# A two-layer convolution kernel: the next load of x moved between the halves of the store, and another order of calls in the first unit

## The chip, the core and the metric

The kernel runs on one core of one Trainium2 chip. The metric is the device time of the whole kernel in microseconds (us), lower is better. The core has five engines that run their own instruction lists and meet only at semaphores: TensorE (PE), VectorE (DVE), ScalarE (ACT), GpSimd (POOL) and SyncE (SP), which here only issues transfers.

## What is computed

The input x is (4, 256, 64, 64), batch, channels, rows, columns. Layer 0 makes 49 attention weights for each pixel from a 7x7 convolution with dilation 2 and a 1x1 convolution behind it, and applies them to the 49 shifted copies of x. Layer 1 adds a gelu term and normalises over the channels.

```python
k = lax.conv_general_dilated(x, w1, window_strides=(1, 1), padding=[(6, 6), (6, 6)], rhs_dilation=(2, 2), dimension_numbers=DN) + b1[None, :, None, None]
k = lax.conv_general_dilated(k, w2, window_strides=(1, 1), padding=[(0, 0), (0, 0)], dimension_numbers=DN) + b2[None, :, None, None]
attn = jax.nn.softmax(k, axis=1)
x = jnp.einsum('bkchw,bkhw->bchw', shifts, attn)          # shifts: the 49 shifted x
y = jax.nn.gelu(yc.T[None, :, None, :] + x * D[None, :, None, None], approximate=False)
out = x + y                                               # then layer norm over the channels
```

yc comes from a scan of 64 steps over a state of 32.

## The kernel before

Dilation 2 lets even and odd rows be treated apart, so the work is cut into 8 units: 4 images times 2 row parities. A unit n is the 32 rows of one parity, with 256 channels as two halves of 128 partitions. x of an even unit lies in raw0, of an odd one in raw1.

The weights are joined first: composite(g) multiplies w2 (relative to the last tap) into row g of w1 on TensorE (14 of them), ScalarE copies five rows in each half (copy_row), VectorE forms sums of rows (row_sums). The convolution over rows is a fast scheme with few products: differences and sums of rows of x (make_u1, make_x1_plus and so on; four of them, c1, c0, c2 and w, on GpSimd) give 11 arrays. Each array is scaled and split in a high fp16 part on ScalarE (v_high) and a low one on VectorE (v_low), into a ring of four slots; the combined weights likewise (weights_high and weights_low, 26 set halves of two instructions each on VectorE). conv(n, first, last) does steps first to last - 1 of 49 on TensorE, 20 matmuls each, seven steps to a block. A block begins only when its arrays are there; in unit 0 (cold) also when its weights are:

```python
if d % DSTEPS == 0:
    pe.wait_ge(vlo, ARRAYS * n + BLOCK_ARRAYS[b])
    if cold:
        pe.wait_ge(w_low, 2 * BLOCK_PARTS[b])
```

The arrays wanted by the seven blocks are 2, 4, 6, 8, 9, 10 and 11, the set halves 4, 8, 12, 16, 20, 24 and 26. The fifth block also waits for the third logit step, the sixth for the fourth.

x is also turned on TensorE (turn_x, eight calls a unit), copied with scale by ScalarE (turned_x) and its low part taken by VectorE (turned_x_low), through two PSUM banks, so turning g waits for low part g - 2. While unit n is convolved, the engines finish unit m = n - 1: logits_i, logits_0 and two turnings of the logits (turn_logits, line 457), softmax, the spread of the attention to bands (spread, line 478), the product of bands and turned x (apply, line 495), gelu, mean and variance, and scale_shift, which completes an output piece and raises the semaphore affine. All orders are written out by hand in each engine's list; an engine that waits blocks what is behind it.

The scale of a unit needs the largest |x|: ScalarE takes it for each half (bound), GpSimd over the partitions (amax), VectorE makes the scales from it (scales). In unit 0 the maximum goes another way, over TensorE.

SP issues the loads and stores. In unit n it waits for the four GpSimd rows and the eight turnings of the old x, loads x of unit n + 1 into the other buffer's place, then stores the four pieces of the unit before (q is the half of the rows, h of the channels) as scale_shift completes them. The pieces with q = 0 are completed late in unit n, those with q = 1 early in unit n + 1. VectorE takes up the new x in make_u1(n + 1) (line 1028), which waits for raw_in.

## Time and profile before

| | |
|---|---|
| median of three runs | 895.67 us (894.84 to 896.17) |
| the profiled execution, device time | 896.21 us |
| its span in the trace | 894.4 us |
| TensorE busy | 803.0 us (90%) |
| VectorE busy | 722.4 us (81%) |
| ScalarE busy | 519.9 us (58%) |
| GpSimd busy | 188.4 us (21%) |
| mean granted TensorE clock | 0.947 |

Times in the trace count from the span's start. Busy time is an average over stages: the first 148 us are the first unit with the weights, then units 1 to 7 follow, and from about 819 us the last unit is finished without a convolution beside it.

### The profile page before, as it was taken

What the parts mean: (1) busy time and instruction counts of PE and PEld (TensorE: products, weight loads), DVE (VectorE), ACT (ScalarE), POOL (GpSimd) and SP (SyncE); (2) the same over time, 40 slices, a digit from 0 to 9 for tenths busy, and PEclk for the clock granted to TensorE, in tenths of its full rate; (3) what the DMA queues carried; (4) which work ended last, traced back from release to release, by engine and by line L of the source; (5) the groups of instructions that cost most, each with busy time, mean ns of one, the idle gap of its engine ahead of it and who ended that gap; (6) DMA issues with size and microseconds to landing.
All of it is one profiled execution on the core that took longest, in us unless ns stands there. A gap on an engine that the chain in (4) does not pass through costs nothing.

```text
span 894.4 us, 27128 instructions
## 1 busy us (share of the span) xinstructions
PE 803.0 (90%) x12261; PEld 493.8 (55%) x12261; DVE 722.4 (81%) x876; ACT 519.9 (58%) x834; POOL 188.4 (21%) x100
## 2 busy tenths in 40 slices
PE   4979787999997999899997999899989999996485
PEld 4975333575555655565564645565546655663451
DVE  3899769889995999689986999599967999677336
ACT  2363232766674666665584767557665659465546
POOL 3114102112510233013311151024301341021010
PEclk9999889999997999999997999999997999999588
DMA  9322005000125010700151011601070011002103
GB/s 312 72 52 45 2 2 95 2 3 2 48 53 92 3 48 2 143 3 1 49 113 33 2 48 42 104 1 40 11 143 2 1 49 50 3 1 64 32 1 94
DMA packets 133597, 41.78 MB, mean 47 GB/s; under 512 B 133145, under 2 KB 133226, under 8 KB 133226
## 3 DMA queue, kind: packets, MB, share of 16 engines
q1 hardware_dynamic: 132248, 40.01, 19.9%
q8 instruction: 96, 1.57, 0.7%
q10 hardware_dynamic: 1234, 0.04, 0.1%
q14 instruction: 19, 0.16, 0.1%
HBM read 23.27 MB, written 16.78 MB: 45 GB/s over the span
## 4 chain that ended last, share of the span: by engine, by line
PE 51%; DVE 15%; issue 12%; ACT 11%; DMA 8%; POOL 1%; SPq 1%; DVEq 0%; ACTq 0%; POOLq 0%
PE cv L438 26%; DMA raw<-in_x_dram 7%; PE wk L495 6%; PE pcomp L603 5%; PE wk L478 4%; PE ms L516 3%; ACT chs L737 3%; ACT V L700 3%; PE wk L529 2%; DVE R L1028 2%; DVE tg L1250 2%; PE wk L457 2%; DVE V L1110 1%; DVE XT L1139 1%; DVE Z L1158 1%
## 5 line engine op out<-in xcount | busy, mean ns | idle before, releaser
L438 PE MATMUL cv<-V,W 128*32 128x496 f16 (+6 forms) x7840 | 447.1, 383 | 19.7 <-issue 7.5
L438 PEld LDWEIGHTS cv<-V,W 128*32 128x32 f16 (+1 forms) x7840 | 201.5, 97 | 224.7 <-issue 41.6
L313 POOL TENSOR_TENSOR R<-raw 128x1152 f32<-128x1152 f32 x32 | 100.2, 3130 | 258.4 <-DVE V L1110 93.8
L700 ACT ACTIVATE V<-R,sc 128x1024 f16<-128x1024 f32 (+1 forms) x88 | 110.5, 1274 | 55.1 <-PE cv L438 54.3
L1110 DVE SCALAR_TENSOR_TENSOR V<-R,sc,V 128x1024 f16<-128x1024 f32 (+1 forms) x88 | 122.4, 1399 | 9.7 <-ACT V L700 9.6
L478 PE MATMUL wk<-AT,sel 128*128 128x16 f16 x2560 | 85.1, 192 | 23.1 <-DVE band L1235 21.2
L495 PE MATMUL wk<-band,XT 128*128 128x224 f16 (+1 forms) x960 | 102.9, 268 | 2.6 <-DVE band L1235 1.4
L478 PEld LDWEIGHTS wk<-AT,sel 128*128 128x128 f16 x2560 | 79.6, 103 | 44.7 <-DVE band L1235 29.6
L495 PEld LDWEIGHTS wk<-band,XT 128*128 128x128 f16 x960 | 83.3, 99 | 25.5 <-issue 5.3
L1235 DVE TENSOR_TENSOR band<-wk,band 128x512 f16<-128x512 f32 x80 | 54.7, 689 | 44.0 <-ACT band L751 43.8
L751 ACT CAST band<-wk 128x512 f16<-128x512 f32 x80 | 46.7, 584 | 69.4 <-PE wk L478 68.4
L731 ACT ACTIVATE XT<-wk,sc 128x512 f16<-128x512 f32 x64 | 42.9, 681 | 53.6 <-PE wk L529 52.9
L760 ACT ACTIVATE o<-wk,sc 128x512 f32<-128x512 f32 x64 | 45.7, 730 | 46.7 <-PE wk L495 46.6
L1041 DVE SCALAR_TENSOR_TENSOR R<-R 128x1024 f32<-128x1024 f32 (+1 forms) x56 | 72.5, 1298 | 0.2
L1028 DVE SCALAR_TENSOR_TENSOR R<-raw 128x512 f32<-128x512 f32 (+1 forms) x48 | 48.2, 1047 | 27.5 <-DMA raw<-in_x_dram 27.4
L1139 DVE SCALAR_TENSOR_TENSOR XT<-wk,sc,XT 128x512 f16<-128x512 f32 x64 | 47.2, 746 | 16.5 <-ACT XT L731 16.3
L338 POOL TENSOR_TENSOR chs<-o 128x1024 f32<-128x1024 f32 x14 | 36.7, 2622 | 110.4 <-DVE o L1256 95.1
L344 POOL TENSOR_TENSOR chs<-tg 128x1024 f32<-128x1024 f32 x14 | 34.5, 2462 | 96.3 <-ACT tg L773 96.3
L603 PE MATMUL pcomp<-w2t,w1raw 128*128 128x48 f32 x196 | 45.0, 418 | 9.4 <-DMA w1raw<-in_L_conv_w_dram 9.4
L1250 DVE SCALAR_TENSOR_TENSOR tg<-o,dcol,yc 128x1024 f32<-128x1024 f32 x32 | 40.4, 1279 | 13.4 <-ACT o L760 13.1
L529 PEld LDWEIGHTS wk<-id,raw 128*128 128x128 f32 x256 | 35.1, 208 | 27.9 <-issue 14.2
L603 PEld LDWEIGHTS pcomp<-w2t,w1raw 128*128 128x128 f32 x196 | 43.7, 312 | 10.0 <-issue 9.6
(138 smaller groups left out, 903.1 us busy)
## 6 DMA issues: line engine op xcount, KB each, us to landing
raw<-in_x_dram SPq DMA_DIRECT2D x16, 1024.0 KB, 11.5
out_dram<-o SPq DMA_DIRECT2D x28, 512.0 KB, 3.9
w1raw<-in_L_conv_w_dram SPq DMA_DIRECT2D x2, 3136.0 KB, 16.8
out_dram<-o SPq DMA_DIRECT2D x8, 256.0 KB, 3.4
cm<-in_L_conv_Cmat_dram ACTq DMA_DIRECT2D x1, 32.0 KB, 8.4
dcol<-in_L_conv_D_dram ACTq DMA_DIRECT2D x2, 0.5 KB, 9.8
lnw<-in_L_conv_ln_w_dram ACTq DMA_DIRECT2D x2, 0.5 KB, 7.2
lnb<-in_L_conv_ln_b_dram ACTq DMA_DIRECT2D x2, 0.5 KB, 7.2
```

What stands on the lines that cost most here:

```text
L313: nc.gpsimd.tensor_tensor(R[buffer][:, :, :, :], rows_of(par, j + 2), rows_of(par, j), ALU.subtract).then_inc(pool_rows, 1)
L438: ins = pe.matmul(to.rearrange("p (w t c) -> p w t c", w=2, c=COLS)[:, :, :, c0:c1], W[:, ws, h * K7 + v, k0:k1], slot(n, a)[:, low, :, t0 ...
L478: ins = pe.matmul(wk[:, r % 2, c * TILES:(c + 1) * TILES].rearrange("p (w j) -> p w j", w=2), sel[:, s, f:f + P], AT[:, :, r:r + 29:4, c], ...
L495: ins = pe.matmul(wk[:, y % 2, (r0 - 16 * q) * COLS:(r1 - 16 * q) * COLS], XT[:, xl, 8 * w + j, h, :], band[:, bl, 8 * w + j, r0 - 4 * j + ...
L603: last = pe.matmul(pcomp[:, g % 3, v * P:v * P + REL], w1h[:, u * K7 + v, :], w2t[:, 0:REL], start=True, stop=True)
L700: nc.scalar.activation(v_array(n, a, 0), array(a), ACT.Identity, scale=sc[:, par, 3:4]).then_inc(vhi, 1)
L1028: nc.vector.scalar_tensor_tensor(out=R[buffer][:, 0:wins, h, :], in0=raw[par][:, h, r:r + 4 * wins - 3:4, :], scalar=-4.0, in1=raw[par][:, ...
L1041: nc.vector.scalar_tensor_tensor(out=part(*out), in0=part(*a), scalar=factor, in1=part(*b), op0=ALU.mult, op1=ALU.add).then_inc(row_made, 1)
L1110: nc.vector.scalar_tensor_tensor(out=v_flat(n, a, 1), in0=array_flat(a), scalar=sc[:, par, 3:4], in1=v_flat(n, a, 0), op0=ALU.mult, op1=AL ...
L1139: nc.vector.scalar_tensor_tensor(out=low, in0=wk[:, g % 2, :], scalar=sc[:, par, 3:4], in1=high, op0=ALU.mult, op1=ALU.subtract).then_inc( ...
L1235: nc.vector.tensor_tensor(band[:, 1, :, r, :], wk[:, r % 2, :].rearrange("p (c t) -> p t c", t=TILES), band[:, 0, :, r, :], ALU.subtract). ...
L1250: nc.vector.scalar_tensor_tensor(out=tg[:, h], in0=o[:, q, h], scalar=dcol[:, h:h + 1], in1=yc[:, h].unsqueeze(1).broadcast_to([P, 16, WID ...
```

## The change

SP: the store is split by q, and the wait and the load of the next x stand between the two halves. TensorE: in unit 0 the turnings of x are spread over the convolution from its start. ScalarE and VectorE: another order of the same calls from the weight products to the second unit. Some waits move from the lists into the functions (sum_copy, bound, inverse_deviation, weights_high, make_u1, logit_scales), and the copy of yc becomes a function. Nothing that is computed changes.

```diff
@@ -273,17 +273,17 @@
                 for h in range(HALVES):
                     sp.dma_start(raw[par][:, h, PAD:PAD + ROWS, :], xv[b, par, h]).then_inc(raw_in[par], 16)
 
-            def store(n, par, b):
-                for q in range(2):
-                    for h in range(HALVES):
-                        sp.wait_ge(affine, 4 * (n - 1) + 2 * q + h + 1)
-                        sp.dma_start(ov[b, 1 - par, h, :, 16 * q:16 * q + 16, :], o[:, q, h]).then_inc(o_free, 16)
-
-            def unit(n, par, b_load, b_out):
+            def store(n, par, b, q):
+
+                for h in range(HALVES):
+                    sp.wait_ge(affine, 4 * (n - 1) + 2 * q + h + 1)
+                    sp.dma_start(ov[b, 1 - par, h, :, 16 * q:16 * q + 16, :], o[:, q, h]).then_inc(o_free, 16)
+
+            def next_load(n, par, b):
+
                 sp.wait_ge(pool_rows, POOL_ROWS * n)
                 sp.wait_ge(xt_done, 8 * n)
-                load(n + 1, 1 - par, b_load)
-                store(n, par, b_out)
+                load(n + 1, 1 - par, b)
 
             sp.dma_start(w2raw[:, :], w2.rearrange("k m a b -> k (m a b)")).then_inc(s_w2, 16)
             for h in range(HALVES):
@@ -292,9 +292,12 @@
                 sp.dma_start(raw0[:, h, PAD:PAD + ROWS, :], xv[0, 0, h]).then_inc(first_in[h], 16)
             sp.wait_ge(s_comp, HALVES * K7)
             load(1, 1, 0)
-            for n in range(1, UNITS - 1):
-                unit(n, n % 2, (n + 1) // 2, (n - 1) // 2)
-            store(7, 1, 3)
+            next_load(1, 1, 1)
+            for n in range(1, UNITS):
+                store(n, n % 2, (n - 1) // 2, 0)
+                if n < UNITS - 2:
+                    next_load(n + 1, (n + 1) % 2, (n + 2) // 2)
+                store(n, n % 2, (n - 1) // 2, 1)
             for i in range(QUARTERS):
                 for h in range(HALVES):
                     sp.wait_ge(q_done[h], i + 1)
@@ -638,11 +641,21 @@
             pe.matmul(pst[LO:LO + TB, 1, 0:1], w2t[:, TA:REL], b1col[:, :], start=True, stop=True).then_inc(s_bsum, 1)
             pe.wait_ge(s_wcp, HALVES * ROW_COPIES)
             pe.wait_ge(s_u, HALVES * ROW_SUMS)
-            conv(0, 0, 16, cold=True)
-            for g in range(8):
-                turn_x(0, 0, g, cold=True)
-                conv(0, 16 + 4 * g, 20 + 4 * g, cold=True)
-            conv(0, 48, CONV, cold=True)
+            turn_x(0, 0, 0, cold=True)
+            turn_x(0, 0, 1, cold=True)
+            conv(0, 0, 6, cold=True)
+            turn_x(0, 0, 2, cold=True)
+            conv(0, 6, 7, cold=True)
+            turn_x(0, 0, 3, cold=True)
+            conv(0, 7, 10, cold=True)
+            turn_x(0, 0, 4, cold=True)
+            conv(0, 10, 16, cold=True)
+            turn_x(0, 0, 5, cold=True)
+            conv(0, 16, 21, cold=True)
+            turn_x(0, 0, 6, cold=True)
+            conv(0, 21, 26, cold=True)
+            turn_x(0, 0, 7, cold=True)
+            conv(0, 26, 49, cold=True)
             pe.wait_ge(s_sel, 15)
             pe.wait_ge(s_const, 2)
             pe.wait_ge(late_cleared, 2)
@@ -704,6 +717,9 @@
                 act.wait_ge(conv_done, NBLOCKS * n + SUM_LAST[s] + 1)
                 if steps:
                     act.wait_ge(z_step, steps)
+                if not n:
+                    act.wait_ge(s_bias, 4)
+                    act.wait_ge(scale_steps, SCALES)
                 add = bias[:, :] if s == M1P else 0.0
                 nc.scalar.activation(dst, summed(n, s), ACT.Identity, bias=add, scale=sc[:, par, 5:6]).then_inc(z_evac, 1)
 
@@ -718,6 +734,9 @@
             def bound(n, par, h):
 
                 act.wait_ge(raw_in[par], 16 * n + (16 if par else 0))
+                if n == 1:
+
+                    act.wait_ge(w_low, 4 * SETS)
                 if h:
                     act.wait_ge(amax_part, 2 * n + 1)
                 elif n >= 2:
@@ -777,6 +796,8 @@
 
             def inverse_deviation(m, q):
                 act.wait_ge(var_done, 2 * m + q + 1)
+                if m == 0 and q == 0:
+                    act.wait_ge(s_const, 2)
                 both = ms[:].rearrange("p a b -> p (a b)")
                 nc.scalar.activation(both, both, ACT.Ln, bias=eps[:, :]).then_inc(ln_done, 1)
                 act.wait_ge(ln_done, 2 * m + q + 1)
@@ -859,6 +880,10 @@
                 turned_x(n, par, 7)
 
             def weights_high(first, last):
+                if first == 0:
+
+                    act.wait_ge(amax_part, 2)
+                    act.wait_ge(s_wscale, 12)
                 for s, h in HIGH_ORDER[first:last]:
                     src, scale, step = weight_source(s, h)
                     if step:
@@ -917,48 +942,48 @@
             copy_row(6)
             scan_copies(5)
             copy_row(7)
-            act.wait_ge(amax_part, 2)
-            act.wait_ge(s_wscale, 12)
-            weights_high(0, 4)
+            weights_high(0, 2)
             copy_row(8)
-            weights_high(4, 8)
+            weights_high(2, 3)
             v_high(0, 0, 0, cold=True)
+            weights_high(3, 4)
             v_high(0, 0, 1, cold=True)
+            weights_high(4, 7)
             copy_row(10)
-            weights_high(8, 12)
+            weights_high(7, 8)
+            v_high(0, 0, 2, cold=True)
+            weights_high(8, 10)
             copy_row(12)
-            weights_high(12, 17)
+            weights_high(10, 11)
             copy_row(13)
-            weights_high(17, 20)
-            v_high(0, 0, 2, cold=True)
-            weights_high(20, 22)
+            turned_x(0, 0, 0)
+            weights_high(11, 12)
             v_high(0, 0, 3, cold=True)
-            act.wait_ge(s_bias, 4)
-            act.wait_ge(scale_steps, 7)
+            weights_high(12, 13)
+            turned_x(0, 0, 1)
+            weights_high(13, 22)
+            turned_x(0, 0, 2)
+            turned_x(0, 0, 3)
             v_high(0, 0, 4)
+            turned_x(0, 0, 4)
+            weights_high(22, 23)
             v_high(0, 0, 5)
-            weights_high(22, 2 * SETS)
-            turned_x(0, 0, 0)
+            weights_high(23, 25)
+            v_high(0, 0, 6)
+            v_high(0, 0, 7)
+            turned_x(0, 0, 5)
             sum_1(0, 0)
-            v_high(0, 0, 6)
-            turned_x(0, 0, 1)
-            v_high(0, 0, 7)
-            turned_x(0, 0, 2)
+            turned_x(0, 0, 6)
             v_high(0, 0, 8)
-            turned_x(0, 0, 3)
-            act.wait_ge(s_const, 2)
-            act.wait_ge(w_low, 4 * SETS)
-            bound(1, 1, 0)
-            turned_x(0, 0, 4)
-            bound(1, 1, 1)
             v_high(0, 0, 9)
             sum_2(0, 0)
-            turned_x(0, 0, 5)
+            weights_high(25, 26)
+            bound(1, 1, 0)
             v_high(0, 0, 10)
-            turned_x(0, 0, 6)
-            turned_x(0, 0, 7)
+            bound(1, 1, 1)
             v_high(1, 1, 0)
             v_high(1, 1, 1)
+            turned_x(0, 0, 7)
             act.wait_ge(late_cleared, 2)
             act.wait_ge(o_free, 64)
             act.preload_act_table_set("natural_log_exp_and_others")
@@ -1044,10 +1069,15 @@
 
 
             def make_u1(n, par):
+                if n <= 1:
+
+                    dve.wait_ge(s_border, 2 * n + 2)
                 if n:
                     dve.wait_ge(raw_in[par], 16 * n + (16 if par else 0))
                     dve.wait_ge(vlo, ARRAYS * n - 2)
                 for h in range(HALVES):
+                    if not n:
+                        dve.wait_ge(first_in[h], 16)
                     u_half(0, par, h, 2, 0, 9)
 
             def make_u0(n, par):
@@ -1127,6 +1157,8 @@
                 dve.wait_ge(scale_steps, SCALES * n + 5)
 
             def logit_scales(n, par):
+                if not n:
+                    dve.wait_ge(s_mask, 2)
                 nc.vector.tensor_scalar(sc[:, par, 4:5], sc[:, par, 1:2], winv[:, :], 1 / X_SCALE, ALU.mult,
                                         ALU.mult).then_inc(scale_steps, 1)
                 dve.wait_ge(scale_steps, SCALES * n + 6)
@@ -1449,6 +1481,11 @@
                                             ALU.add).then_inc(s_bias, 1)
                 dve.wait_ge(s_bias, 4)
 
+            def copy_yc():
+                dve.wait_ge(s_yc, 1)
+                nc.vector.tensor_copy(yc[:, :, :], pst[:, 0, 0:HALVES * WIDTH].rearrange(
+                    "p (h w) -> p h w", h=HALVES)).then_inc(normed, 4)
+
             nc.vector.memset(b2col[:, :], 0.0).then_inc(s_b2z, 1)
             nc.vector.memset(mask[0:3 * TILE, :], 1.0).then_inc(s_mask, 1)
             nc.vector.memset(mask[3 * TILE:P, :], 0.0).then_inc(s_mask, 1)
@@ -1467,9 +1504,6 @@
             row_sums(5)
             row_sums(6)
             weight_scales()
-            for h in range(HALVES):
-                dve.wait_ge(first_in[h], 16)
-            dve.wait_ge(s_border, 2)
             make_u1(0, 0)
             make_u0(0, 0)
             x_maximum_row()
@@ -1477,72 +1511,73 @@
             make_x1_minus(0)
             x_maximum_all()
             scales(0, 0)
-            dve.wait_ge(s_mask, 2)
             logit_scales(0, 0)
+            weights_low(0, 1)
+            make_u2(0, 0)
             row_sums(8)
-            weights_low(0, 2)
+            make_y1_plus(0)
+            row_sums(9)
             v_low(0, 0, 0)
-            row_sums(9)
+            weights_low(1, 2)
             v_low(0, 0, 1)
-            weights_low(2, 4)
+            weights_low(2, 3)
+            make_y1_minus(0)
             row_sums(11)
-            make_u2(0, 0)
-            make_y1_plus(0)
             row_sums(12)
-            make_y1_minus(0)
-            weights_low(4, 6)
             row_sums(13)
+            weights_low(3, 4)
+            make_x2_plus(0)
+            copy_yc()
+            make_x2_minus(0)
+            v_low(0, 0, 2)
+            v_low(0, 0, 3)
+            turned_x_low(0, 0, 0)
             relative_bias()
-            v_low(0, 0, 2)
-            weights_low(6, 8)
-            v_low(0, 0, 3)
-            make_x2_plus(0)
-            make_x2_minus(0)
-            weights_low(8, 12)
+            turned_x_low(0, 0, 1)
+            weights_low(4, 11)
+            turned_x_low(0, 0, 2)
             v_low(0, 0, 4)
+            weights_low(11, 12)
+            turned_x_low(0, 0, 3)
+            weights_low(12, 14)
+            make_y2_plus(0)
             v_low(0, 0, 5)
-            make_y2_plus(0)
+            turned_x_low(0, 0, 4)
+            v_low(0, 0, 6)
+            weights_low(14, 15)
             make_y2_minus(0)
-            weights_low(12, 16)
             make_q2(0)
-            turned_x_low(0, 0, 0)
-            v_low(0, 0, 6)
-            turned_x_low(0, 0, 1)
             v_low(0, 0, 7)
+            weights_low(15, 18)
+            make_q3(0)
+            weights_low(18, 19)
+            make_q1(0)
             fold_1(0, 0)
+            turned_x_low(0, 0, 5)
             logits_1(0, 0)
-            turned_x_low(0, 0, 2)
-            weights_low(16, 20)
-            make_q3(0)
-            make_q1(0)
+            turned_x_low(0, 0, 6)
             v_low(0, 0, 8)
-            turned_x_low(0, 0, 3)
-            weights_low(20, 2 * SETS)
-            turned_x_low(0, 0, 4)
+            weights_low(19, 21)
+            make_u1(1, 1)
+            weights_low(21, 22)
+            make_u0(1, 1)
+            weights_low(22, 26)
             v_low(0, 0, 9)
-            dve.wait_ge(s_yc, 1)
-            nc.vector.tensor_copy(yc[:, :, :], pst[:, 0, 0:HALVES * WIDTH].rearrange(
-                "p (h w) -> p h w", h=HALVES)).then_inc(normed, 4)
             logits_2(0, 0)
+            logits_rows(0, True)
+            make_x1_plus(1)
+            scales(1, 1)
             v_low(0, 0, 10)
-            dve.wait_ge(s_border, 4)
-            make_u1(1, 1)
-            make_u0(1, 1)
-            make_x1_plus(1)
+            logit_scales(1, 1)
             make_x1_minus(1)
-            logits_rows(0, True)
+            make_u2(1, 1)
             logits_rows(0, False)
-            scales(1, 1)
-            logit_scales(1, 1)
-            turned_x_low(0, 0, 5)
-            turned_x_low(0, 0, 6)
-            turned_x_low(0, 0, 7)
-            make_u2(1, 1)
             v_low(1, 1, 0)
             make_y1_plus(1)
+            logits_d(0, 0)
             make_y1_minus(1)
             v_low(1, 1, 1)
-            logits_d(0, 0)
+            turned_x_low(0, 0, 7)
             dve.wait_ge(late_cleared, 2)
             dve.wait_ge(s_d_in, 32)
             dve.wait_ge(normed, 4)
```

## Rows read from the trace of the kernel before

**Rows 1.** Waits over the span: who waited for whom, us in total, times, longest.

```profile
DVE R L1028 <- DMA raw<-in_x_dram: 27.4, 5, 5.9
```

**Rows 2.** TensorE in order of time: start, length; second turnings of units 1, 2 and 7.

```profile
156.11 1.09 PE L457 MATMUL wk<-id,Z 128*128 128x128 f32 x8
...
248.06 1.09 PE L457 MATMUL wk<-id,Z 128*128 128x128 f32 x8
...
734.67 1.09 PE L457 MATMUL wk<-id,Z 128*128 128x128 f32 x8
```

**Rows 3.** VectorE in order of time, first use of next x, units 1 and 3.

```profile
181.72 1.42 DVE L1028 SCALAR_TENSOR_TENSOR R<-raw 128x576 f32<-128x576 f32 x2
...
376.64 1.43 DVE L1028 SCALAR_TENSOR_TENSOR R<-raw 128x576 f32<-128x576 f32 x2 [5.43 <-DMA raw<-in_x_dram]
```

**Rows 4.** TensorE in order of time, end of unit 2 and within unit 3.

```profile
332.38 0.74 PE L529 MATMUL wk<-id,raw 128*128 128x128 f32 x4
...
378.73 2.10 PE L478 MATMUL wk<-AT,sel 128*128 128x16 f16 x64 [4.47 <-DVE band L1235]
380.75 2.33 PE L438 MATMUL cv<-V,W 128*32 128x496 f16 x20
```

**Rows 5.** Chain that ended last, unit 3: start, length, what.

```profile
362.18 2.53 SPq L274
...
364.76 11.86 DMA raw<-in_x_dram
```

**Rows 6.** TensorE in order of time, unit 0 and start of unit 1.

```profile
67.41 19.49 PE L438 MATMUL cv<-V,W 128*32 128x512 f16 x320 [5.29 <-issue]
...
95.74 4.97 PE L438 MATMUL cv<-V,W 128*32 128x512 f16 x60 [2.06 <-DVE V L1110]
...
139.63 5.39 PE L438 MATMUL cv<-V,W 128*32 128x480 f16 x100
148.01 4.88 PE L438 MATMUL cv<-V,W 128*32 128x512 f16 x60 [2.99 <-DVE Z L1149]
...
157.14 14.78 PE L438 MATMUL cv<-V,W 128*32 128x480 f16 x280
```

**Rows 7.** Stretches: length, busy by engine (instructions), granted clock, DMA share, GB/s.

```profile
47.80:147.20 99.40, 79.89 (x1081) 46.12 (x1080) 82.59 (x134) 38.65 (x51) 16.95 (x10) 0.95 0.21 36
...
97.00:98.00 1.00, 1.00 (x16) 0.48 (x12) 0.98 (x2) 0.00 (x0) 0.00 (x0) 0.50 0.06 16
144.02:158.02 14.00, 11.01 (x156) 5.60 (x152) 13.62 (x14) 2.34 (x3) 6.24 (x2) 0.88 0.64 105
```

**Rows 8.** VectorE in order of time, unit 0.

```profile
61.98 3.67 DVE L1436 SCALAR_TENSOR_TENSOR W<-ut,wsc,W 128x224 f16<-128x224 f32 x4
65.58 1.73 DVE L1367 SCALAR_TENSOR_TENSOR ut<-pcomp,ut 128x336 f32<-128x336 f32 x4
...
67.79 1.28 DVE L1110 SCALAR_TENSOR_TENSOR V<-R,sc,V 128x1024 f16<-128x1024 f32 x1
...
76.05 2.51 DVE L1436 SCALAR_TENSOR_TENSOR W<-ut,wsc,W 128x224 f16<-128x224 f32 x8
...
108.98 0.74 DVE L1139 SCALAR_TENSOR_TENSOR XT<-wk,sc,XT 128x512 f16<-128x512 f32 x1
```

**Rows 9.** GpSimd in order of time, units 0 and 1.

```profile
62.14 2.77 POOL L313 TENSOR_TENSOR R<-raw 128x1152 f32<-128x1152 f32 x1 [29.82 <-DVE R L1036]
...
107.86 3.69 POOL L313 TENSOR_TENSOR R<-raw 128x1152 f32<-128x1152 f32 x1 [22.74 <-issue]
119.78 0.37 POOL L309 PARTITION_ALL_REDUCE aall<-amx  x1 [8.22 <-ACT tg L725]
...
197.00 2.87 POOL L313 TENSOR_TENSOR R<-raw 128x1152 f32<-128x1152 f32 x1 [7.24 <-issue]
```

**Rows 10.** ScalarE in order of time, unit 0.

```profile
60.60 0.44 ACT L884 COPY wc<-pcomp 128x336 f32<-128x336 f32 x1 [0.30 <-PE pcomp L603]
...
115.17 1.91 ACT L725 ACTIVATE tg<-raw 128x2048 f32<-128x2048 f32 x1 [8.08 <-DVE W L1436]
```

## The prediction, made before the change was run

> **What bounds the kernel now.** I read three things in this order: who waits for whom over the whole run, then TensorE in order of time, then the other engines around the two places where TensorE stands still. The first view shows one wait that has no business in an engine-bound kernel: VectorE waits five times, 27.4 us in all, for the load of x [rows 1]. TensorE's order of time cuts the run into eight units. The second turning of the logits is a mark that every unit from 1 to 7 passes: 156.11, 248.06 and, for unit 7, 734.67 [rows 2]. So unit 1 lasts 248.06 - 156.11 = 91.95 us, and units 2 to 6 together 734.67 - 248.06 = 486.61, or 97.3 each. The difference, 5.4 us each, is what the reader should see first.
>
> In unit 3 VectorE comes to the first rows of the next x and stands 5.43 us for the transfer; unit 1 has no wait at the same instruction [rows 3]. TensorE is the second to stand, 4.47 us for a band that VectorE owes, and its next convolution step takes 2.33 us, about 1.1 more than usual [rows 4]. The chain says why: the load is issued only at 362.18, behind the last piece of the store, and takes another 11.86 us to land after its second half is out [rows 5]. Its buffer had been free far earlier: the last turning of the old x ends at 332.38 + 0.74 = 333.12 [rows 4].
>
> The second place is the first unit. TensorE begins its convolution at 67.41 after standing 5.29, and before unit 1 starts at 148.01 it stands again and again, 2.06 and 2.99 us in the rows shown [rows 6]. Meanwhile VectorE, from 47.80 to 147.20, is busy 82.59 of 99.40 us [rows 7].
>
> **The load of x, part by part.** No transfer is added or removed. SP now waits for the first half of the store, then for the old x to be done, issues the load, and then waits for the second half. The load of unit 4 would go out at 333.2 in place of 362.2; SP's issue and the flight together took 376.62 - 362.18 = 14.4 us [rows 5], so it lands near 348. VectorE wants it at 371 (376.64 less the 5.43) [rows 3]: 23 us of cover. If that cover were gone, the wait of 5.43 would be back. Queued behind the load is the second half of the store, whose values come in the next unit, 20 us after the load is issued; its price is nothing. The wait that now stands on SP before that half (for the turning) ends at 333.12, before that second half is ready, so it holds nothing up.
>
> What unit 2 to 6 then look like is not a guess, since unit 1 is a unit whose next load came early: it ran between 144 and 158, with a DMA share of 0.64, while VectorE went on at 13.62 of 14.00 us [rows 7]. Taking unit 1's 91.95 for the five gives 459.75 and saves 26.9. The high end is VectorE's whole 27.4 and 1.1 for each of five slow steps, 33. The low end is the 4.47 of TensorE's stop in five units, 22. I take 27, the row of a whole unit.
>
> **The first unit: its start.** TensorE may begin when the last row sums are done, at 65.58 + 1.73 = 67.31 now. In the new list VectorE reaches them after 3 half-products of the weights instead of 6, and the GpSimd difference that is released by the fourth combination (62.14, 2.77 us) no longer meets weight products: those four instructions took 3.67 where eight take 2.51 undisturbed, a stall of 2.4 [rows 8, 9]. It now meets row sums, which read PSUM with one operand, as the low part of a turned x does; that one kept its 0.74 at 108.98 while a difference ran [rows 8, 9]. Fourteen us of work stand between 47.80 and the last row sums, so they wait for the copy of the last composite row, 60.60 + 0.44 [rows 10]. Their end is then near 63.2: TensorE begins 4.2 us earlier, and stands 1 us instead of 5.29.
>
> **The first unit: its end.** From there TensorE has 49 steps at 14.78 / 14 = 1.05 us [rows 6] and eight turnings at 0.7: 57 us, done by 120. VectorE has more. Both lists hold the same instructions up to the second low part of unit 1 (the last turned x goes after it, the MD sum before it, 0.75 each). So its sum is the 82.59 busy us [rows 7]. Of these about 9 are stalls on GpSimd (an estimate: four differences fall on such instructions, at 2.4 each, and the last begins beside the 0.74 from PSUM, so it costs less). Walking the new list, the four differences meet: row sums (0), a low part that goes first (0.75), a turned x and then a low part (2.0), and logits from PSUM (0): 2.75 in all. 47.80 + 82.59 - 9 + 2.75 = 124.1. Walking instruction by instruction with 1.25 for a low part and 0.31 for a weight product [rows 8], and each wait on ScalarE, TensorE or GpSimd, I come to 126.0. Its stations: first six steps of the convolution from 64.5 (the turnings of x 0 and 1 go first, they need no copy), low products for the second block 73.9, low parts 2 to 5 of V by 82.6 (third block), low parts 6 and 7 by 90.9 (fourth), turned x 5 at 97.3, low products for the fifth block 101.6, all low products 107.9, low part 9 at 109.3 (sixth block after the M2 fold, 110.2), low part 10 at 116.3, last block 117.6 to 125.0. ScalarE keeps ahead of each: of its moved calls, the maxima of the next x wait for all low products, until 107.9, and only the tenth high part and the maximum behind them wait for it. The walk shows where TensorE then waits: half a us at the second block, 0.6 at the third, 1.4 and 1.3 at the fifth and sixth. None is as long as the 2.06 before 95.74, after which the granted clock is 0.50 (1.2 GHz) in the stretch from 97 to 98 [rows 6, 7]. Unit 1 begins at 126 instead of 148.01. VectorE then owes the last turned x, the MI sum, one low part behind a GpSimd difference and the M0 sums, 5.4 us, where TensorE has 3.3: a stop of 2 that before was hidden by a convolution at half clock (4.88 for three steps [rows 6]). The mark of unit 1 comes at 126 + 5.4 + 3.3 = 134.7 instead of 156.11: 21.4 saved. A walk finds no stall that it does not know of, and the stop of 2 may cost a half-clock stretch, 1.6 by the first three steps of unit 1 (4.88 against 3.2), so I take 19. The bounds: 22 above, 12 below.
>
> The new waits in the lists (first x, masks, weights all low before ScalarE takes the maximum of the next x) stood beside the same calls before, or are met long before: nothing.
>
> One cost the trace does not settle. Scales of unit 1 now stand ahead of the low part for the seventh block, so TensorE waits for GpSimd's maximum over partitions. ScalarE's two maxima take 1.91 each [rows 10] and end near 113.3. The reduction's row says 0.37 us, but the next GpSimd instruction comes only after 7.24 us of "issue" [rows 9]. If the result is out at the end of the 0.37, the scales are ready at 113.9 and VectorE comes at 114.2: nothing. If it is out only after the 7.6, VectorE stands until 121, TensorE stands 5.7 at the last block and restarts at half clock: 6.9 in all. I take the row at its word, since the idle time lies after it. The Trainium skill, "GPSIMD Engine Reference", section Instruction dispatch, says that the first call of a freshly loaded kernel pays about 6 us of code load with no instruction visible in the profile. By that rule the 6 us could stand before the result; this trace has an unseen gap of that size, but behind the reduction.
>
> **Sum.** The profiled execution took 896.21 (span 894.4): 896.21 - 19 - 27 = 850.2. The median of the runs is 0.5 below it: 850.
>
> **Rivals.**
> (a) *The maximum over partitions is slow, or VectorE's list slips as much otherwise*: for it the 7.24 us gap, against it the row's own 0.37. 850 + 7 = 857.
> (b) *Only one half pays.* Either the five stops are replaced by another wait (877: the first unit alone), for which ScalarE's and GpSimd's share of the next unit would have to be late, and unit 1 speaks against it; or the reordered first unit gives nothing (869), for which VectorE's order would have to starve TensorE's blocks.
> (c) *Slower than before.* The early load runs beside the start of each unit. If it slowed TensorE there, the kernel would be slower from 46 / 5 = 9.2 us a unit on, 60% on the 14.78 of that stretch; at 100% it would be 850 + 5 x 14.78 = 924. Against it: while unit 2's load began, TensorE ran 5 steps in 5.39 [rows 6], 1.08 each against 1.05.
> (d) *The order of SP changes nothing*, since the transfer is hidden or late anyway: the 5.43 us wait excludes "hidden", the 23 us of cover "late"; it is part of (b).
>
> **Chances and range.** Forecast 0.66 (842 to 855), (a) 0.19 (855 to 862), (b) 0.11 (862 to 880), (c) 0.02, below 842 0.02. The range 842 to 862 takes in the bounds 896.21 - 22 - 33 - 0.5 = 841 (nearly) and 896.21 - 12 - 22 - 0.5 = 862, and leaves out 0.15. No change means within 0.2%, 1.8 us, about what this kernel's runs can tell: 0.01. Faster 0.97, slower 0.02.
>
> **What would show it.** No VectorE wait for x in units 2 to 6; six equal periods of 91 to 92; load issued about 1 us after the last turning; a granted clock of 1.00 at the place of the stop in units 2 to 6. First convolution at 64 to 65, no TensorE stop over 2.1 us before 126, VectorE with almost no idle from 48 to 126. The scales of unit 1 within 1 us of the reduction's end show (a) wrong; a stop of 5 or 6 us before the last block shows it right. Wrong would be a unit 1 mark later than 145, or periods above 93.

## The result, and the profile after

The changed kernel takes 846.38 us (median of four runs, 845.74 to 846.7) against 895.92 of the kernel before, run beside it (894.84 to 899.35): the ratio is 0.944, with a 95% interval of 0.9414 to 0.9466. Forecast were 850.0 and a range of 842 to 862. TensorE's mean granted clock rose from 0.947 to 0.978.

The page of the profile after: the span, the busy times, and the granted clock in 40 slices of the span (in tenths of full speed).

```profile
span 844.8 us, 27130 instructions
...
PE 787.0 (93%) x12261; PEld 490.8 (58%) x12261; DVE 719.2 (85%) x876; ACT 518.4 (61%) x834; POOL 190.9 (23%) x100
...
PEclk9999999999999999999999999999999999998588
```

TensorE has as many instructions as before and 16.0 us less busy time (803.0 before). The same steps ran at a higher clock: that is the part of the gain that a count of stops alone misses.

The waits over the span have no line for the load of x any more; VectorE's longest entry is this one (us in total, times, longest).

```profile
DVE band L1267 <- ACT band L770: 42.2, 52, 4.9
```

TensorE in order of time: the second turnings of units 1, 2 and 7, and the last turning of x in unit 1 with the seven steps behind it. They answer to [rows 2, 4].

```profile
134.25 1.09 PE L460 MATMUL wk<-id,Z 128*128 128x128 f32 x8 [0.22 <-DVE chs L1242]
...
213.08 0.74 PE L532 MATMUL wk<-id,raw 128*128 128x128 f32 x4
213.75 7.48 PE L441 MATMUL cv<-V,W 128*32 128x496 f16 x140
...
226.23 1.09 PE L460 MATMUL wk<-id,Z 128*128 128x128 f32 x8
...
685.27 1.09 PE L460 MATMUL wk<-id,Z 128*128 128x128 f32 x8
```

The first mark went from 156.11 to 134.25, so the first unit gave 21.86 us. Unit 1 lasts 226.23 - 134.25 = 91.98, as before. Units 2 to 6 take 685.27 - 226.23 = 459.04 in place of 486.61, 27.57 less. Together that is 49.43 of the 894.4 - 844.8 = 49.6 that the span lost: nothing of note changed elsewhere.

The five periods behind unit 1 are not quite equal: four last 91.97 to 92.01, the one of unit 6 lasts 685.27 - 594.17 = 91.10. Its mark, and the sums u0 that VectorE forms in it:

```profile
594.17 1.09 PE L460 MATMUL wk<-id,Z 128*128 128x128 f32 x8
```

```profile
634.77 1.28 DVE L1053 SCALAR_TENSOR_TENSOR R<-raw 128x512 f32<-128x512 f32 x2
```

In the other five units of 1 to 6 these sums take 3.72 to 3.77, because GpSimd's difference c1 begins beside them. In unit 6 it began only at 635.51, when they were more than half done. The experiments at the end are about this meeting.

The transfers' queue: the first half of the store, then the next load. The load is that of unit 3's x; VectorE's first use of it, in unit 2, answers to the waiting row of [rows 3].

```profile
209.54 3.48 SPq L280 DMA_DIRECT2D out_dram<-o  x2
213.90 5.29 SPq L274 DMA_DIRECT2D raw<-in_x_dram  x2
```

```profile
251.84 1.42 DVE L1053 SCALAR_TENSOR_TENSOR R<-raw 128x576 f32<-128x576 f32 x2
```

The load goes out at 213.90, just after the turning that ends at 213.08 + 0.74 = 213.82, and VectorE comes to it 38 us later with no wait.

The first unit on TensorE, against [rows 6].

```profile
62.77 1.96 PE L532 MATMUL wk<-id,raw 128*128 128x128 f32 x8 [0.90 <-DVE ut L1399]
64.66 7.65 PE L441 MATMUL cv<-V,W 128*32 128x512 f16 x120
...
101.49 7.48 PE L441 MATMUL cv<-V,W 128*32 128x512 f16 x140 [1.07 <-DVE V L1140]
109.84 14.78 PE L441 MATMUL cv<-V,W 128*32 128x512 f16 x280 [0.87 <-DVE ev L1181]
125.74 3.29 PE L441 MATMUL cv<-V,W 128*32 128x512 f16 x60 [1.12 <-DVE V L1140]
130.66 1.09 PE L460 MATMUL wk<-id,Z 128*128 128x128 f32 x8 [1.64 <-DVE Z L1181]
131.68 2.35 PE L441 MATMUL cv<-V,W 128*32 128x496 f16 x40
```

Unit 1 now begins at 125.74 and its first three steps take 3.29; before it was 148.01 and 4.88. No stop in that stretch is above 1.12, and the largest behind it is 1.64.

VectorE and GpSimd in the first unit: the row sums, a low part of V that meets a GpSimd difference, the maximum over partitions, the scales made from it.

```profile
58.74 3.89 DVE L1399 SCALAR_TENSOR_TENSOR ut<-pcomp,ut 128x336 f32<-128x336 f32 x8
...
84.36 2.25 DVE L1140 SCALAR_TENSOR_TENSOR V<-R,sc,V 128x1024 f16<-128x1024 f32 x1 [0.90 <-ACT V L713]
...
114.13 0.21 DVE L1146 TENSOR_SCALAR sc<-aall 128x1 f32<-128x1 f32 x1 [0.27 <-POOL aall L312]
```

```profile
112.86 1.24 POOL L312 PARTITION_ALL_REDUCE aall<-amx  x1 [14.18 <-ACT tg L744]
```

Stretches of the kernel after (columns as in [rows 7]): the first unit, the first 2.3 us of its convolution, the seven steps of the fifth block (beside the load of unit 2's x), and seven steps beside the load of unit 3's x.

```profile
47.50:125.40 77.90, 73.99 (x1081) 45.84 (x1080) 74.44 (x134) 39.85 (x55) 16.49 (x10) 1.00 0.32 56
...
64.70:67.00 2.30, 2.30 (x25) 0.88 (x28) 2.30 (x3) 2.30 (x4) 0.02 (x1) 1.00 1.35 217
...
102.00:109.00 7.00, 6.97 (x136) 3.73 (x128) 6.97 (x16) 1.32 (x1) 0.00 (x0) 1.00 1.36 220
214.00:221.00 7.00, 7.00 (x140) 3.47 (x132) 6.14 (x8) 5.11 (x5) 3.40 (x3) 1.00 1.13 218
```

VectorE is busy 74.44 of 77.90 us, 96%, where it had 82.59 of 99.40; the same 134 instructions take 8.15 us less. The mean granted clock of this stretch is 1.00.

### The profile page after: what moved, and what is told of

It is laid out like the page before. It is cut to its first block, busy times and chain, and to the rows that moved or that the text cites. A ratio compares the mean times of both kernels' runs of the same rounds, so it can differ in the third digit from the quotient of the medians.

```text
span 844.8 us, 27130 instructions
## 1 busy us (share of the span) xinstructions
PE 787.0 (93%) x12261; PEld 490.8 (58%) x12261; DVE 719.2 (85%) x876; ACT 518.4 (61%) x834; POOL 190.9 (23%) x100
## 4 chain that ended last, share of the span: by engine, by line
PE 55%; DVE 23%; issue 13%; ACT 6%; DMA 1%; POOL 1%; DVEq 0%; SPq 0%; ACTq 0%; POOLq 0%
PE cv L441 32%; PE wk L481 7%; PE pcomp L606 5%; DVE tg L1282 3%; PE ms L519 3%; DVE Z L1190 3%; PE wk L532 3%; DVE R L1053 3%; DVE V L1140 2%; PE wk L498 2%; DVE XT L1171 2%; DVE R L1061 2%; DVE Z L1181 1%; PE wk L460 1%; ACT tg L744 1%
## 5 line engine op out<-in xcount | busy, mean ns | idle before, releaser
L441 PE MATMUL cv<-V,W 128*32 128x496 f16 (+6 forms) x7840 | 429.7, 373 | 3.1 <-DVE V L1140 2.2
L441 PEld LDWEIGHTS cv<-V,W 128*32 128x32 f16 (+1 forms) x7840 | 198.6, 96 | 197.9 <-issue 11.3
L1066 DVE SCALAR_TENSOR_TENSOR R<-R 128x1024 f32<-128x1024 f32 (+1 forms) x56 | 70.3, 1256 | 0.2
L785 ACT ACTIVATE tg<-tg 128x1024 f32<-128x1024 f32 x32 | 33.9, 1058 | 31.6 <-DVE tg L1282 30.6
L1053 DVE SCALAR_TENSOR_TENSOR R<-raw 128x512 f32<-128x512 f32 (+1 forms) x48 | 52.9, 1144 | 0.0
```

Source lines behind the costliest of these rows:

```text
L441: ins = pe.matmul(to.rearrange("p (w t c) -> p w t c", w=2, c=COLS)[:, :, :, c0:c1], W[:, ws, h * K7 + v, k0:k1], slot(n, a)[:, low, :, t0 ...
L1053: nc.vector.scalar_tensor_tensor(out=R[buffer][:, 0:wins, h, :], in0=raw[par][:, h, r:r + 4 * wins - 3:4, :], scalar=-4.0, in1=raw[par][:, ...
L1066: nc.vector.scalar_tensor_tensor(out=part(*out), in0=part(*a), scalar=factor, in1=part(*b), op0=ALU.mult, op1=ALU.add).then_inc(row_made, 1)
```

## The experiments

Marks are those of [rows 2]: the start of the second turning in a unit. Two profiles of the same list can differ by up to 1 us in them (unit 1: 156.11 and 155.14 with the old lists, 133.88 to 135.22 with the new); where this matters it is taken off.

**The two halves apart.** The first kernel has only the new order of SP on top of the kernel before; the second is the changed kernel with SP's old order. The edit of the first (that of the second undoes it):

```diff
-            for n in range(1, UNITS - 1):
-                unit(n, n % 2, (n + 1) // 2, (n - 1) // 2)
-            store(7, 1, 3)
+            next_load(1, 1, 1)
+            for n in range(1, UNITS):
+                store(n, n % 2, (n - 1) // 2, 0)
+                if n < UNITS - 2:
+                    next_load(n + 1, (n + 1) % 2, (n + 2) // 2)
+                store(n, n % 2, (n - 1) // 2, 1)
```

> The kernel before with the new order of SP alone: load between the halves of the store, all engine lists as before. My theory: the two halves of the change add up. Unit 1 keeps its mark near 156, the waits of VectorE for x in units 2 to 6 are gone, the five units take 91.9 us each, and the device time is 896 - 27 = 869 us (867 to 871). Rival: the early load only pays after the reordered first unit, or another wait follows it in the old lists; then it saves under 20 us (876 or more).

> The changed kernel with the old order of SP: the four pieces of the store before the load. My theory: the first unit saves its 22 us by itself (mark of unit 1 at 134 to 135), the five waits for x stay at 5 us each, and the device time is 896 - 22 = 874 us (872 to 876). Rival: the earlier unit 1 shifts the late load too, so that the waits grow or shrink by more than 1 us each (under 870 or over 880).

The first took 868.03 us (ratio 0.9675, 0.9647 to 0.9704): no wait for x, all periods from 91.9 to 92.0, the unit 1 mark at 155.14, 1 us from the 156.11 of before. The second took 873.98 us (0.9755, 0.972 to 0.979), with the mark at 133.88 and the old wait, in its waits over the span:

```profile
DVE R L1050 <- DMA raw<-in_x_dram: 27.5, 5, 5.7
```

The spans are 894.4 - 865.9 = 28.5 and 894.4 - 871.5 = 22.9 shorter. Their sum, 51.4, is within 2 us of the 49.6 of both: the halves add up, and neither feeds the other. By the marks the fit is closer: in the first kernel units 2 to 6 take 706.95 - 247.12 = 459.83, 26.78 less than before, and in the second the unit 1 mark is 22.23 earlier, together 49.0.

**How late may the load be?** The load goes behind the first of the two late store pieces instead of ahead of both.

```diff
                 store(n, n % 2, (n - 1) // 2, 0)
+                store(n, n % 2, (n - 1) // 2, 1, (0,))
                 if n < UNITS - 2:
                     next_load(n + 1, (n + 1) % 2, (n + 2) // 2)
-                store(n, n % 2, (n - 1) // 2, 1)
+                store(n, n % 2, (n - 1) // 2, 1, (1,))
```

> The changed kernel with the load issued after three pieces of the store, one piece earlier than the kernel before, where the third piece came 3 us before the fourth. Theory (the gain is exactly the wait that the late load causes): the load starts 3 us earlier than before, so VectorE still stands 2 to 2.5 us in each of units 2 to 6, and the device time is 846.4 + 5 x 2.3 = 858 us (856 to 861). Rival (the load in the next unit is what costs, beside the wait, by its traffic): over 864. Rival (any place before the last piece will do): 846 to 848.

859.57 us (0.9575, 0.9541 to 0.9608). The waits, and VectorE in unit 2:

```profile
DVE R L1054 <- DMA raw<-in_x_dram: 13.0, 5, 2.9
```

```profile
253.23 1.43 DVE L1054 SCALAR_TENSOR_TENSOR R<-raw 128x576 f32<-128x576 f32 x2 [2.56 <-DMA raw<-in_x_dram]
```

One store piece ahead of the load costs half of the wait, 13.0 of 27.4, and 859.57 - 846.38 = 13.2 us of time; by the marks units 2 to 6 take 696.95 - 224.97 = 471.98, 12.94 more than in the changed kernel and 12.15 more than the 459.83 above. So the wait really was the queue place behind the two late pieces, and each us that VectorE waits costs about one us of time. TensorE's stops for bands are fewer: 21.2 us in the kernel before, 9.0 in this one.

**The first unit: the GpSimd difference beside weight products.** One product pair is moved from ahead of the difference to beside it, ahead of the last row sums.

```diff
+            weights_low(3, 4)
             row_sums(11)
             row_sums(12)
             row_sums(13)
-            weights_low(3, 4)
```

> The changed kernel with one weight product of VectorE moved ahead of three groups of row sums, to where GpSimd's difference is released. Theory (the two engines exclude each other when VectorE reads two SBUF operands, not when it reads PSUM): the product's second instruction ends only with the difference, 2.3 us late, TensorE begins at 65.5 instead of 62.8, and since VectorE's list sets the first unit, the mark of unit 1 and the device time are 2.3 us later (848.7, 848 to 849.5). Rival (the order before row sums is free): 0.0 to 0.6 us.

849.38 us (0.9464, 0.9437 to 0.949). VectorE:

```profile
58.13 3.05 DVE L1468 SCALAR_TENSOR_TENSOR W<-ut,wsc,W 128x224 f16<-128x224 f32 x2
...
61.94 3.65 DVE L1399 SCALAR_TENSOR_TENSOR ut<-pcomp,ut 128x336 f32<-128x336 f32 x8
```

The difference ran from 58.29 for 2.76. The product pair beside it took 3.05, in the changed kernel 0.69: a stall of 2.36. The eight row sums took 3.65 without a difference beside them and 3.89 with one, so they pay nearly nothing. TensorE's first convolution began at 67.62 in place of 64.66, and the mark came at 137.05, 2.8 later: 2.36 for the stall, and the rest is within what two profiles differ by. The prediction's "stall of 2.4" has its size, and the row sums are where it isn't paid.

**Who sets the first unit?** Two reductions that nobody reads are put on VectorE in the middle of the unit, behind the last low products; in another kernel the last turning of x is done four times, on TensorE.

```diff
+            def extra(k):
+                for i in range(k):
...
+                    nc.vector.tensor_reduce(spare[:, :], raw1[:, 0, PAD:PAD + 16, :].rearrange("p r w -> p (r w)"), AX,
+                                            ALU.max).then_inc(s_extra, 1)
...
+            extra(2)
```

```diff
-            turn_x(0, 0, 7, cold=True)
+            turn_x(0, 0, 7, cold=True, times=4)
```

> The changed kernel with two idle maxima over 1024 columns of x added to VectorE's list in the first unit, ahead of the tenth low part of V (their result is not used). My theory: VectorE sets the first unit, so both, about 1.1 us each, appear in full: mark of unit 1 at 136.5 instead of 134.25, device time 848.6. Rival (TensorE sets it): the mark moves by less than 0.5 us.

> The changed kernel with the last turning of x in the first unit done four times over by TensorE, 12 transposes and 2.1 us more. My theory: TensorE has stops of 1.07, 0.87 and 1.12 us behind it before unit 1 begins, so the 2.1 us vanish in them: mark of unit 1 moved by 0 to 0.3 us, device time 846.4 to 846.7. Rival (TensorE sets the first unit): 2.1 us later, 848.5.

With VectorE's work 849.29 us (0.9489, 0.9473 to 0.9505), with TensorE's 846.95 (0.946, 0.9446 to 0.9474). TensorE, in the first and the second of them:

```profile
98.24 0.74 PE L534 MATMUL wk<-id,raw 128*128 128x128 f32 x4 [0.26 <-DVE XT L1173]
...
113.06 19.56 PE L443 MATMUL cv<-V,W 128*32 128x512 f16 x340 [3.38 <-DVE ev L1183]
```

```profile
97.00 2.19 PE L532 MATMUL wk<-id,raw 128*128 128x128 f32 x16 [0.26 <-DVE XT L1171]
...
108.38 15.71 PE L441 MATMUL cv<-V,W 128*32 128x464 f16 x293 [0.36 <-issue]
```

The reductions took 2.47 on VectorE; the stop at the sixth block grew from 0.87 to 3.38, and the mark moved by 3.07. Of that 0.71 was there before the edit (the turning at 98.24, in the changed kernel 97.53), so 2.47 of VectorE's work cost 2.36. On TensorE 2.19 - 0.74 = 1.45 us more in one row (I had counted on 2.1) left the mark where it was (133.71, this profile having been 0.53 early already): the stop at the fifth block, 1.07, is gone and that at the sixth shrank from 0.87 to 0.36. VectorE sets the first unit.

**The stop behind the start of unit 1.** The M0 sums go ahead of the low part that meets a GpSimd difference.

```diff
             def unit(n, par, nxt=True):
                 m, other = n - 1, 1 - par
                 logits_i(m, other)
-                v_low(n, par, 2)
+                if m:
+                    v_low(n, par, 2)
                 logits_0(m, other)
+                if not m:
+                    v_low(n, par, 2)
```

> The changed kernel with one exchange on VectorE, in unit 1 only: the M0 sums of the logits ahead of the third low part, which there runs into GpSimd's difference (2.37 instead of 1.28 us). Theory: TensorE's stop of 1.64 us at the first turning of the logits goes, the mark of unit 1 comes 1.6 us earlier (132.6), device time 844.8. Rival: the low part is then missed by a later block or the softmax chain, and nothing is won.

844.5 us (0.9437, 0.9423 to 0.9451). TensorE:

```profile
129.04 1.09 PE L460 MATMUL wk<-id,Z 128*128 128x128 f32 x8
...
132.36 1.09 PE L460 MATMUL wk<-id,Z 128*128 128x128 f32 x8
```

Both stops, 1.64 and 0.22, are gone and the mark is 1.89 earlier. The medians differ by 1.9 too, though the intervals of the two ratios overlap; the marks are the evidence here. The two kernels at the end of this section are another pair with and without this exchange; there the medians, 836.4 and 838.31, differ by 1.9 with runs that don't overlap.

**The stop that is left in every unit.** In units 1 to 6 TensorE still stands 0.87 before the third turning of x, for the low part of the first (VectorE). Here one convolution step is put ahead of that turning.

```diff
                 turn_x(n, par, 1)
+                conv(n, 37, 38)
                 turn_x(n, par, 2)
-                conv(n, 37, 40)
+                conv(n, 38, 40)
```

> The changed kernel with one step of the convolution moved on TensorE, in all units, from behind the third turning of x to ahead of it, so that the wait of 0.86 us for the first low part of turned x (units 1 to 5, 0.56 in unit 6) is covered. Theory (units are now bound by TensorE alone): 4.9 us less, device time 841.5. Rival (VectorE's chain through the maxima and gelu is as long as TensorE's list): the wait returns at the next turning, 0 to 1 us less.

845.68 us (0.9448, 0.9433 to 0.9462): my gain of 4.9 did not come. TensorE in unit 2:

```profile
294.91 1.98 PE L519 MATMUL ms<-chs,ones 128*128 128x512 f32 x4 [0.75 <-POOL chs L347]
```

The stop moved to the variance, which waits for GpSimd's sum of squares, which waits for VectorE's centred rows: the period of unit 2 is 318.30 - 226.32 = 91.98 as before. Unit 1 came out shorter (91.10), but not by this edit: in it c1 happened to start 0.79 behind the start of u0 (in unit 2 it was 0.09), and u0 took 1.28, just as in unit 6 of the changed kernel. The mark of unit 7 is where it was, 685.28 against 685.27, so the 0.7 between the medians shows no gain. The stop at the turning was only where VectorE's lateness showed first.

**Taking work off VectorE's path.** In the changed kernel GpSimd's difference c1 starts 7.22 us behind the maximum over partitions and meets VectorE's differences u0. In unit 1, on VectorE and on GpSimd:

```profile
174.83 3.73 DVE L1053 SCALAR_TENSOR_TENSOR R<-raw 128x512 f32<-128x512 f32 x2
```

```profile
175.12 2.89 POOL L316 TENSOR_TENSOR R<-raw 128x1152 f32<-128x1152 f32 x1 [7.22 <-issue]
```

So c1 was put ahead of the maximum, alone and with the M0 sums first.

```diff
                 if nxt:
-                    amax(n + 1, 1 - par)
                     make_c1(n + 1, 1 - par)
+                    amax(n + 1, 1 - par)
```

> The changed kernel with one exchange on GpSimd, in units 1 to 6: the difference c1 of the next x ahead of the maximum over partitions. c1 starts 7.2 us after the maximum now and holds VectorE's next two halves of u0 back (3.77 us where 1.3 would do); the early load makes it possible from about 26 us after the unit's mark, where VectorE works on bands in PSUM. Theory (a unit is now set by VectorE and TensorE alike, so two us off VectorE's list free TensorE's stops of 0.86 and 0.24 us, and no more): 1.0 to 1.1 us less for each of six units, device time 840.4 (839.5 to 841.5). Rival (VectorE is then held by ScalarE's copies and gelu, the time is given back in the same unit): 0 to 2 us less in all.

> Both exchanges that looked promising: the M0 sums first in unit 1 and c1 ahead of the maximum in units 1 to 6. Theory: they touch different units, so they add up: 1.9 us (measured) and 6 us less than the changed kernel, device time 838.5 (837.5 to 840).

Both are slower than the changed kernel's 846.38: 860.24 us (0.9634, 0.9591 to 0.9676) and 855.95 (0.9563, 0.9541 to 0.9584). The profile of the first is that of its slowest run, 868.91; the others took 858.45 to 861.21. Its unit 1, on VectorE, on TensorE, and by stretches:

```profile
160.53 3.87 DVE L1053 SCALAR_TENSOR_TENSOR R<-raw 128x576 f32<-128x576 f32 x2
...
179.68 1.28 DVE L1053 SCALAR_TENSOR_TENSOR R<-raw 128x512 f32<-128x512 f32 x2
```

```profile
165.06 2.09 PE L481 MATMUL wk<-AT,sel 128*128 128x16 f16 x64 [1.56 <-DVE band L1267]
167.08 2.11 PE L441 MATMUL cv<-V,W 128*32 128x496 f16 x20
...
171.16 2.19 PE L441 MATMUL cv<-V,W 128*32 128x480 f16 x20
...
174.34 4.87 PE L441 MATMUL cv<-V,W 128*32 128x464 f16 x60
```

```profile
165.00:170.00 5.00, 4.93 (x113) 3.40 (x114) 2.74 (x5) 3.07 (x4) 0.19 (x1) 0.73 0.02 5
170.00:180.00 10.00, 10.00 (x161) 5.32 (x158) 7.11 (x10) 3.58 (x5) 0.18 (x1) 0.62 0.01 2
```

u0 is free now (1.28), but u1 pays in its place (3.87 for what takes 1.42), and behind u1 stands a low part of a band for which TensorE waits. TensorE stops 1.56, and the convolution steps behind the stop take 2.11, 2.19 and 4.87 where the changed kernel has 1.27, 1.20 and 3.29. That is 3.4 us for the clock, 1.56 for the stop, and 1.46 saved (next experiment): 3.5 a unit, and the measured period is 230.46 - 134.93 = 95.53, 3.55 more. By the median the price is less, (860.24 - 846.38) / 6 = 2.3 a unit, and the second kernel shows where it varies. TensorE in its unit 1:

```profile
162.65 2.09 PE L481 MATMUL wk<-AT,sel 128*128 128x16 f16 x64 [1.55 <-DVE band L1267]
164.67 2.25 PE L441 MATMUL cv<-V,W 128*32 128x496 f16 x20
```

The stop is the same, but only one step is slow; the next takes 1.20 again (granted clock 0.83 from 165 to 170, 1.00 from 170 to 180). That gives 1.55 + 0.98 - 1.46 = 1.1 for the unit, measured 225.62 - 132.50 = 93.12, 1.14 more. Its unit 2 has two slow steps (2.33 and 2.19) and lasts 94.37. So the stop comes in every unit, and how long the clock stays low behind it differs.

**The same difference, held back to where VectorE reads PSUM.** The wait is new against the last two kernels.

```diff
                 if nxt:
+                    pool.wait_ge(blo, 10 * m + 6)
                     make_c1(n + 1, 1 - par)
                     amax(n + 1, 1 - par)
```

> The difference c1 of GpSimd goes ahead of the maximum of the next x, as in the two kernels before, but now it waits for the last low band of the unit, so that it runs beside low parts of bands whose other operand is in PSUM; the M0 sums also go ahead in the first unit. Theory A: what spoiled the two kernels before was only where c1 began (beside the sums u1, with the band's low part behind them). Then the stop of 1.56 us and the half clock behind it are gone, the period falls below 91.98, by up to the 0.86 and 0.24 us stops of a unit: 838 to 842. Theory B: GpSimd in that place meets VectorE's two-operand work again somewhere in the unit: the period stays at 92 or above it, 844.5 (the M0 sums alone) or more, and 850 or more if a stop again brings half clock.

> The same gated place of c1 with the first unit as in the changed kernel. Theory A: 1.9 us above the kernel with the M0 sums first, so 840 to 844. Theory B: 846.4 or more.

836.4 us (835.57 to 837.56; 0.9355, 0.9332 to 0.9378) with the M0 sums first, 838.31 (838.06 to 838.81; 0.9377, 0.9354 to 0.9399) without. Theory A held, and both gains were above what I gave it (838 to 842, and 840 to 844). In the former, VectorE and GpSimd in unit 1, and the marks of units 1 and 2:

```profile
173.24 1.28 DVE L1054 SCALAR_TENSOR_TENSOR R<-raw 128x512 f32<-128x512 f32 x2
```

```profile
163.84 2.66 POOL L316 TENSOR_TENSOR R<-raw 128x1152 f32<-128x1152 f32 x1 [19.37 <-DVE band L1268]
172.35 0.37 POOL L312 PARTITION_ALL_REDUCE aall<-amx  x1 [5.85 <-issue]
```

```profile
132.63 1.09 PE L461 MATMUL wk<-id,Z 128*128 128x128 f32 x8
...
223.15 1.09 PE L461 MATMUL wk<-id,Z 128*128 128x128 f32 x8
```

The period is 90.52 in place of 91.98; c1 takes 2.66, u0 1.28 instead of 3.73, and the stop at the third turning is gone (0.19 is left before the variance). The unit 7 mark is at 675.74: six periods gave 551.02 - 543.11 = 7.9 and the first unit 134.25 - 132.63 = 1.6, together the 9.5 between the spans of 844.8 and 835.3 us. The chain of work that ended last says the same, first the changed kernel, then this one:

```profile
PE 55%; DVE 23%; issue 13%; ACT 6%; DMA 1%; POOL 1%; DVEq 0%; SPq 0%; ACTq 0%; POOLq 0%
```

```profile
PE 74%; issue 10%; DVE 7%; ACT 4%; POOL 3%; DMA 1%; DVEq 0%; SPq 0%; ACTq 0%; POOLq 0%
```

In unit 1 of this kernel the 0.19 is TensorE's only stop: its own list now sets nearly all of the period.

## Why the prediction was right, and where it was off

**The load of x.** Forecast 26.9 from unit 1's period; by the marks it measured 26.78 for this half alone and 27.57 in the changed kernel. In the latter 0.88 is luck, unit 6 with its 91.10. Each step held: issue within 1 us of the last turning (0.08), 38 us to its first use, no wait behind the load for the late store pieces. The sum of VectorE's five waits, 27.4, would have been as good a price as the row of a whole unit. TensorE's stops, 21.2 in all for bands, are too low a price, since slow steps stand behind them. The forecast's high end, the waits and 1.1 for each slow step, counted the slow steps twice: 27.4 us of waits cost 26.78 or 27.57 and, with one store piece late, 13.0 cost 12.2 to 12.9, slow steps included.

**The first unit's start.** Forecast 63.2 for TensorE and 64.5 for the first convolution; measured 62.77 and 64.66. The "stall of 2.4" that the row sums avoid measured 2.36.

**The first unit's end.** The walk gave 126.0 for the start of unit 1 and 134.7 for its mark; measured 125.74 and 134.25. The stops came at the places walked: 1.07 for 1.4 at the fifth block, 0.87 for 1.3 at the sixth, 1.12 for 1.0 at unit 1, 1.64 + 0.22 for "a stop of 2". The stops of 0.5 and 0.6 at the second and third blocks did not appear; the first six steps were 1.3 us slow (7.65 against 6 x 1.05), which used up that room. VectorE's stalls on GpSimd, put at 2.75 behind 47.80, come to 1.2: 0.24 at the row sums and 0.97 at the low part at 84.36 (2.25 for 1.28); at the other low part GpSimd was the one that waited (3.64 for 2.64). The 9 for the old list was right: 82.59 - 74.44 + 1.2 = 9.35. That VectorE sets this stretch was argued there and is shown by the reductions (2.36 of 2.47 paid) and the repeated turning (nothing paid).

**Where it was off.** The result is 3.6 below the forecast. The step that was mis-sized is "so I take 19": from a walk that gave 21.4 I took 2.4 off, 1.6 of it for a stretch at half clock behind the stop of 2, the rest for slips. Neither came. The clock stayed at 1.00 behind the 1.64, and the first unit gave 21.86: 2.9 of the 3.6. The load's term of 27 was 0.6 low, which is less than the 0.88 that chance gave in unit 6.

**The rivals.** (a), the slow maximum over partitions, is refuted: the record ends at 112.86 + 1.24 = 114.10 and VectorE starts on the result at 114.13. The row's own length (1.24, not the 0.37 of [rows 9]) was off, but behind ScalarE's second maximum it cost only the 0.27 of VectorE's wait. The Trainium skill, "GPSIMD Engine Reference", section Instruction dispatch, would have let about 6 us without a visible instruction stand before the result; here it did not stand there. (b) is refuted by the two halves alone, which give 28.5 and 22.9 us of span. (c) is refuted beside the loads: with DMA shares of 1.36 (102 to 109) and 1.13 (214 to 221) seven steps take 7.48, against 14.78 / 2 = 7.39 in a stretch of fourteen. (d) fell with (b).

**What the experiments corrected.** Twice I took a stop of TensorE for a gain that a changed order would bring, and was wrong. Moving TensorE's turning moved the stop; moving c1 freely moved the stall to a worse place. Only giving VectorE back its 2.45 us a unit, without taking them elsewhere, shortened the period. That c1's meeting with VectorE's differences was the cause of the 91.98 is shown by that kernel and by its twin without the M0 sums. The units in which the two missed each other by chance say it without any edit: 91.10 in unit 6 of the changed kernel, and 91.10 and 91.09 in unit 5 of the kernels with more TensorE and more VectorE work.

## What to carry to other kernels

Price a removed wait by a whole period of a stage that never had it. Here the summed wait of VectorE, the engine that waits for the transfer, was as good; the stops that it causes on TensorE were not, for the slow steps behind a stop come on top, and adding those to VectorE's wait counts them twice. When a stop on the bounding engine vanishes on reordering and returns elsewhere, the engine that owes it has as much to do as the engine that bounds the unit: free time there. And look at every unit of a trace, not at one: a unit that is shorter without an edit is an experiment that costs nothing. On VectorE and GpSimd, choose by hand which pair of instructions meets: a difference on GpSimd that began beside VectorE's work on two SBUF inputs cost VectorE 2.4 us in each of the three places looked at (2.36, 2.45, 2.45), and 0.2 or nothing where VectorE read one input from PSUM.

## What the runs showed of the hardware that was not expected

- What VectorE pays for meeting a difference is about what is left of the difference. A low part that began at 84.36, 1.48 us into one, took 2.25 in place of 1.28. Where VectorE was first, the difference took 3.64 at 66.98 in place of 2.64 and VectorE paid nothing.
- A stop of 1.56 us was followed by granted clocks of 0.73 (165 to 170) and 0.62 (170 to 180) in the kernel with c1 first, and the convolution steps behind it took 2.11 and 2.19 in place of 1.27 and 1.20. A stop of 1.64 us in the first unit of the changed kernel was followed by steps at full speed (2.35 for two), and behind 1.55 in the kernel with both exchanges one step was slow (2.25) and the next took 1.20. The length of a stop alone does not decide it; what does was not tried.
- The first six steps of the convolution took 7.65 us, 1.3 more than six later ones, though the granted clock reads 1.00: 25 matmuls in the 2.30 us from 64.70, beside a DMA share of 1.35. The transfer alone is not the cause, since seven steps took 7.48 beside a DMA share of 1.36 (102 to 109). The cause stays open.
- GpSimd has an unseen gap between a difference and the maximum over partitions where one directly follows the other: 7.22 us behind the maximum in unit 1 (6.93 to 7.15 in units 2 to 5), and 5.85 ahead of it where the difference comes first. What it is was not tried. The result isn't held up by the gap behind it; a maximum that directly follows a difference is late by the gap ahead of it. In the fastest kernel that was hidden, since the scales were wanted later.
